# Moving the denominator step, the transposes and the query/key/value weight loads in a fused linear-attention and gated-FFN layer

## What is computed

```
qkv = x @ w_qkv;  q = elu(q) + 1;  k = elu(k) + 1;  kv = k * v
run_kv_f, run_ks_f = decay_scan(kv, a), decay_scan(k, a)      # out[t] = a*out[t-1] + in[t]
run_kv_s, run_ks_s = decay_scan(kv, b), decay_scan(k, b)
den_f = clip(sum_over_head(q * run_ks_f), 1e-6);  den_s = the same with run_ks_s
att = concat(q * run_kv_f / den_f, q * run_kv_s / den_s) @ w_out
y   = layernorm(x + att)
out = layernorm(y + (silu(y @ wg.T) * (y @ wu.T)) @ wd.T)     # wg, wu, wd: int32 / 127
```

## Time and profile before

| what | us |
|---|---|
| median of 3 runs | 2980.36 |
| lowest and highest of them | 2740.66, 2985.13 |
| the profiled execution | 2740.66 |
| its span on the slowest core | 2739.1 |
| spans of all cores | 2712.3 to 2739.1 |

### The profile page before, as it was taken

One profiled execution on the slowest core, in us unless ns is written; L12 is line 12 of the kernel. 1 busy time (PEld: TensorE's weight loads), 2 busy tenths in 40 slices (PEclk: granted clock), 3 DMA queues, 4 the chain that ended last, 5 costly groups with the idle time before them and its releaser, 6 DMA issues.

```text
span 2739.1 us, 21184 instructions; the slowest of 8 cores (2712.3 to 2739.1 us)
## 1 busy us (share of the span) xinstructions
PE 1753.3 (64%) x7153; PEld 726.9 (27%) x7298; DVE 833.9 (30%) x1010; ACT 525.3 (19%) x576; POOL 384.8 (14%) x308
## 2 busy tenths in 40 slices
PE   0222253788567883778567883778467883878586
PEld 0000011333222331333223331333123331333232
DVE  0122204342334313342334313342334313441111
ACT  0011102221113202221113212221123112221111
POOL 6411111111012101111021101111121101120000
PEclk9655567899888996899889996999789996999898
DMA  8999983424733273323633263323532273314433
GB/s 111 127 126 128 125 146 101 132 76 101 164 115 100 64 175 88 128 80 96 169 115 100 70 170 121 101 73 110 156 131 85 76 196 102 103 58 147 134 104 112
DMA packets 259467, 316.06 MB, mean 115 GB/s; under 512 B 91171, under 2 KB 173092, under 8 KB 257060
## 3 DMA queue, kind: packets, MB, share of 16 engines
q1 hardware_dynamic: 175396, 235.00, 29.4%
q0 software_dynamic: 7168, 46.15, 12.9%
q10 hardware_dynamic: 76800, 33.57, 5.7%
HBM read 318.80 MB, written 54.53 MB: 136 GB/s over the span
## 4 chain that ended last, share of the span: by engine, by line
PE 45%; DVE 16%; ACT 10%; DMA 8%; POOL 7%; issue 6%; another core or an unknown queue 6%; ACTq 1%; SPq 0%; DVEq 0%; POOLq 0%
DVE runs L529 11%; PE C_ps L722 8%; PE A_ps L391 8%; PE D_ps L722 6%; POOL denr L408 4%; DMA wo_buf<-wo_s 4%; PE C_ps L776 3%; PE D_ps L776 3%; PE A_ps L776 3%; PE B_ps L776 3%; POOL runs L551 3%; PE B_ps L391 2%; ACT sgb L732 2%; PE C_ps L599 2%
## 5 line engine op out<-in xcount | busy, mean ns | idle before, releaser
L722 PE MATMUL C_ps<-y1T,wg_buf 128*128 128x512 bf16 x1506 | 379.3, 406 | 202.6 <-ACT sgb L732 131.0
L391 PE MATMUL A_ps<-xT,wq_buf 128*128 128x512 bf16 x1003 | 280.2, 438 | 168.6 <-DMA wq_buf<-wq_s 132.9
L551 POOL TENSOR_TENSOR runs<-qb,runs 128x1024 f32<-128x1024 f32 x64 | 148.7, 2345 | 1420.2 <-DVE states_sb L538 1420.2
L722 PE MATMUL D_ps<-y1T,wu_buf 128*128 128x512 bf16 x1504 | 344.6, 379 | 3.4 <-DVE hbuf L739 0.3
L420 PE MATMUL B_ps<-denr,bones_sb 128*128 128x512 bf16 x124 | 57.3, 556 | 450.4 <-POOL denr L408 450.4
L739 DVE TENSOR_TENSOR hbuf<-D_ps,sgb 128x1024 bf16<-128x1024 f32 x96 | 117.6, 1225 | 562.7 <-ACT sgb L732 562.7
L722 PEld LDWEIGHTS C_ps<-y1T,wg_buf 128*128 128x128 bf16 x1536 | 152.5, 103 | 426.7 <-issue 284.7
L732 ACT ACTIVATE sgb<-C_ps,cv_sb 128x1024 bf16<-128x1024 f32 x96 | 107.0, 1114 | 565.2 <-PE D_ps L722 401.1
L391 PEld LDWEIGHTS A_ps<-xT,wq_buf 128*128 128x128 bf16 x1024 | 111.3, 111 | 341.6 <-issue 265.0
L722 PEld LDWEIGHTS D_ps<-y1T,wu_buf 128*128 128x128 bf16 x1536 | 149.0, 98 | 187.1 <-issue 10.0
L391 PE MATMUL B_ps<-xT,wq_buf 128*128 128x512 bf16 x504 | 124.9, 402 | 47.5 <-DMA wq_buf<-wq_s 47.0
(11 more groups left out here) (79 smaller groups left out, 1494.1 us busy)
## 6 DMA issues: line engine op xcount, KB each, us to landing
wq_buf<-wq_s SPq DMA_DIRECT2D x192, 256.0 KB, 3.6
wg_buf<-wg_s SPq DMA_DIRECT2D x192, 256.0 KB, 3.0
wu_buf<-wu_s SPq DMA_DIRECT2D x192, 256.0 KB, 4.3
wd_buf<-wd_s SPq DMA_DIRECT2D x384, 128.0 KB, 2.2
wo_buf<-wo_s SPq DMA_DIRECT2D x256, 128.0 KB, 3.5
out<-work ACTq DMA_DIRECT2D x64, 256.0 KB, 6.0
xbf<-x POOLq DMA_DIRECT2D x32, 256.0 KB, 185.6
xbm<-xbf POOLq DMA_DIRECT2D x32, 256.0 KB, 4.6
```

The costliest lines, as they stand in the source:

```text
L391: t.matmul(o, a, b, start=f1, stop=f2),
L551: lambda v, q_=qv, r_=kvpart: v.tensor_tensor(r_.rearrange("p (o t) -> p o t", o=2), q_, r_.rearrange("p (o t) -> p o t", o=2), OP.mult),
L722: t.matmul(o, a, b, start=f1, stop=f2),
```

## The change

1. `emit_den` moves out of `emit_A` to the level of the subtiles. A pair no longer runs its denominator step at the head of the next pair's segment; it is put into a list `den_q`, and `pop_den()` takes it from there: behind gate steps 2, 6 and 10 for pairs 0, 1 and 2, and between the two halves of stage D for pair 3. In stage A of subtile 0 it is called behind every second segment, which is the old order.
2. The call of `next` behind the additions of line 618 goes. The first two segments (matmuls of pair 0, scans of pair 0) come behind the whole first layer norm.
3. The loads of wq are issued by POOL (`q="gpsimd"`) and not by SP. The first three chunks stand ahead of the `xbm` loads.
4. The transposes of x and of y1 are issued by SP and not by ACT. Those of y1 come behind all of the layer norm, and the first chunks of wg and wu stand between the second and the third of them.
5. The waits of the second half of stage D on `A_ps` and `B_ps` are read when that half is emitted, so that they take in the denominator step of pair 3.

```diff
     def emit_A(sg):
         s, st = divmod(sg, NST)
+        for ci in range(3):
+            stream_chunk2(sg, "wq", wq_buf, wq_s, wq_in, wq_slot_g,
+                          wq_cval, ci, q="gpsimd")
         emit_xcast(sg)
         for c in range(NCH):
...
-            prog.op("scalar",
+            prog.op("sync",
                     lambda s_, d=dview, z=sview: s_.dma_start(
                         out=d, in_=z, transpose=True),
...
-        for ci in range(3):
-            stream_chunk2(sg, "wq", wq_buf, wq_s, wq_in, wq_slot_g,
-                          wq_cval, ci)
...
             if mi % 2 == 1 and ci + 3 < 12:
                 stream_chunk2(sg, "wq", wq_buf, wq_s, wq_in, wq_slot_g,
-                              wq_cval, ci + 3)
+                              wq_cval, ci + 3, q="gpsimd")
...
-        pend = [None]
         for pr in range(NJ // 2):
-            if pend[0] is not None:
-                emit_den(*pend[0])
-                pend[0] = None
...
-            pend[0] = (pr, qp, v_q, v_scans, num_vals)
+            den_q.append((pr, qp, v_q, v_scans, num_vals))
             yield
-        emit_den(*pend[0])
-        pend[0] = None
         g["xT"] = ch_m.n
-        yield
...
         g["xbm_v"] = ch_v.n
-        if a_next_gen is not None:
-            next(a_next_gen, None)
...
+        y1t_tr(2)
+        y1t_tr(3)
+        stream_chunk2(sg, "wg", wg_buf, wg_s, wg_in, wg_slot_g, wg_cval, 0)
+        stream_chunk2(sg, "wu", wu_buf, wu_s, wu_in, wu_slot_g, wu_cval, 0)
+        y1t_tr(0)
+        y1t_tr(1)
+        for ci in range(1, 3):
             stream_chunk2(sg, "wg", wg_buf, wg_s, wg_in, wg_slot_g,
                           wg_cval, ci)
...
             if mp in (1, 3, 5, 7, 9) and a_next_gen is not None:
                 next(a_next_gen, None)
+            if mp in (2, 6, 10):
+                pop_den()
...
             if h2 == 0:
                 gPS["C"] = [("v", ch_v.n)]
                 gPS["D"] = [("v", ch_v.n)]
+                pop_den()
+                if a_next_gen is not None:
+                    next(a_next_gen, None)
```

More of the change, by code:

```diff
@@ L290, in stream_chunk2 @@
         mi0 = 2 * ci
[L291 to L307, removed]
+        rdy = [conv_ready[key][mi0], conv_ready[key][mi0 + 1]]
+        assert all(r is not None for r in rdy), (key, mi0)
+        for a in range(2):
+            dst2 = buf[:, sl * 2048 + a * 1024: sl * 2048 + (a + 1) * 1024]
+            prog.op(q,
+                    lambda s, d=dst2, z=scratch[mi0 + a]:
+                        s.dma_start(out=d, in_=z),
+                    waits=rdy + [(ch_m, slot_g[sl])],
+                    inc=wch, inc_n=16)
         cval[ci] = (wch, wch.n)
@@ L354, in emit_xcast, with emit_den @@
         return ch_xc.n
+    def emit_den(pr, qp, v_q, v_scans, num_vals):
+        for jj in range(2):
+            j = 2 * pr + jj
+            qv = qb[qp][:, jj * 512:(jj + 1) * 512].rearrange(
+                "p (o t) -> p o t", o=1).broadcast_to([128, 2, 512])
+            kvpart = runs[:, jj * 2048: jj * 2048 + 1024]
+            kspart = runs[:, jj * 2048 + 1024: jj * 2048 + 2048]
+            v_dr = prog.op(
+                "gpsimd",
+                lambda v, q_=qv, r_=kspart: v.tensor_tensor(
+                    denr.ap().rearrange("p (o t) -> p o t", o=2), q_,
+                    r_.rearrange("p (o t) -> p o t", o=2), OP.mult),
+                waits=[(ch_v, v_scans), (ch_v, v_q),
+                       (ch_m, g["denr"])], inc=ch_p)
+            wB2 = [(chof(t), v) for t, v in gPS["B"]]
+            m_d = None
+            for dec in range(2):
+                m_d = prog.op(
+                    "tensor",
+                    lambda t, o=B_ps[:, dec * 512:(dec + 1) * 512],
+                    r_=denr[:, dec * 512:(dec + 1) * 512]:
+                        t.matmul(o, bones_sb[:], r_, start=True,
+                                 stop=True),
+                    waits=([(ch_p, v_dr)] + (wB2 if dec == 0 else [])),
+                    inc=ch_m if dec == 1 else None, inc_n=2)
+            g["denr"] = ch_m.n
+            v_cl = prog.op("vector",
+                           lambda v: v.tensor_scalar(
+                               denc[:], B_ps[:], 1e-6, None, OP.max),
+                           waits=[(ch_m, m_d), (ch_v, g["denc"])],
+                           inc=ch_v)
+            gPS["B"] = [("v", v_cl)]
+            v_ln = prog.op("scalar",
+                           lambda s_: s_.activation(denc[:], denc[:],
+                                                    AF.Ln),
+                           waits=[(ch_v, v_cl)], inc=ch_s)
+            v_ex = prog.op("scalar",
+                           lambda s_: s_.activation(
+                               denc[:], denc[:], AF.Exp,
+                               scale=cvap("neg1")),
+                           waits=[(ch_s, v_ln)], inc=ch_s)
+            num_val = num_vals[jj]
+            cview = concat.ap().rearrange(
+                "p (d e t) -> p d e t", d=2, e=NJ)[:, :, j, :]
+            v_of = prog.op(
+                "vector",
+                lambda v, o=cview, r_=kvpart: v.tensor_tensor(
+                    o, r_.rearrange("p (o t) -> p o t", o=2),
+                    denc.ap().rearrange("p (o t) -> p o t", o=2),
+                    OP.mult),
+                waits=[(ch_s, v_ex), (ch_m, g["concat"]),
+                       (ch_p, num_val)],
+                inc=ch_v)
+            g["denc"] = v_of
+            g["concat_ready"] = v_of
+        g["runs"] = ch_v.n
+        g_q[qp] = ch_v.n
@@ L681, in emit_BCD @@
                 g_stat[wl] = ch_v.n
[L682 to L692, removed]
         if a_next_gen is not None:
@@ L695, in emit_BCD, with y1t_tr @@
             next(a_next_gen, None)
-        for ci in range(3):
+        def y1t_tr(c):
+            dview = y1T.ap().rearrange("p (j t) -> p j t", j=NJ)[
+                :, :, c * 128:(c + 1) * 128]
+            sview2 = y1b[:, c * DM:(c + 1) * DM].rearrange(
+                "p (j f) -> p j f", j=NJ)
+            prog.op("sync",
+                    lambda s_, d=dview, z=sview2: s_.dma_start(
+                        out=d, in_=z, transpose=True),
+                    waits=[(ch_v, y1vals[c]), (ch_m, g["y1T"])],
+                    inc=ch_yt, inc_n=16)
+        y1t_tr(2)
[5 more added lines that the diff above has]
+        for ci in range(1, 3):
             stream_chunk2(sg, "wg", wg_buf, wg_s, wg_in, wg_slot_g,
@@ L701, in emit_BCD @@
                           wu_cval, ci)
+        yt_val = ch_yt.n
+        g["xbm_yt"] = ch_yt.n
         for mp in range(NMI_F // 2):
@@ L768, in emit_BCD @@
                     if k == 0 and c == 0:
-                        w = w + firstD[h2]
+                        keys = ("C", "D") if h2 == 0 else ("A", "B")
+                        w = w + [(ch_v, h_done)] + [
+                            (chof(t), v) for key in keys for t, v in gPS[key]]
                     prog.op(
@@ L865, in build_nc @@
     a_gen = emit_A(0)
-    run_gen(a_gen)
+    _SENT = object()
+    nseg = 0
+    while next(a_gen, _SENT) is not _SENT:
+        nseg += 1
+        if nseg % 2 == 0:
+            pop_den()
+    while den_q:
+        pop_den()
     for sg in range(N_SUBTILES):
```

13 lines of the change are left out of this document (8 added, 5 removed).

## The result

| | before | changed |
|---|---|---|
| median of 11 runs, us | 2806.73 | 2676.23 |
| lowest to highest | 2734.33 to 2985.13 | 2672.29 to 2951.17 |
| profiled execution | 2740.66 | 2674.31 |
| ratio, with 95% interval | 1 | 0.9776 (0.9761 to 0.9792) |

The change makes the kernel 2.2% faster. Some runs of both kernels are a few per cent longer than the rest, with a lower granted clock on some of the cores; the ratio leaves these out, and so does all that follows. The forecast was 2639, or 3.7% under the profiled execution of the kernel before: the sign is right, the time 35 us too low, inside the range of 2570 to 2725.

What follows compares the result with a forecast made beforehand. The prediction took the kernel to be bound by PE and its waits, chiefly 450.4 us for `denr`. It summed 2740.66 + 132 (start) - 234 (seven periods) = 2639 us, range 2570 to 2725.

Steps and rivals of the forecast that it cites:

- The start: Subtile 0: wq loads wait behind POOL's conversions, first matmul at 350, first wout ends at 541.6 and not 409.7: +132 us.
- Without SP's 9.4% the queue is 36 us shorter: At the start: POOL's queue, without SP's share beside it, runs dry at 348 and not 384.4 us.
- The period: Each of seven equal stretches after the first wout: 271.8 us against 305.2, 234 us gained over seven.
- wout to first gate step: In each period: 24 us, bounds 22 and 38, from transposes of x there at +14 and y1T at +20 to +24.
- gate steps 0 and 1: In each period: 6.9 + 2.6 (wait for Silu) + 6.9 = 16.4 us; scans end before gate step 1 needs `D_ps`.
- two middle segments: In each period: pair matmuls, gate step, denominator, three gate steps; 52.8 us each, 105.6 together, hardly less than before.
- last segment: In each period: ends at the product of gate step 11, which stage D waits for; 13.4 + 6.9 + 17.7 = 38.0 us.
- wait between them: Stage D, between its halves: the second half waits until `B_ps` is clipped twice; a new wait of 10.5 us.
- 192 matmuls, 41.5 + 1: Stage D, both halves, in each period: 42.5 us of matmuls.
- Loads served at once: Rival for the start: wq loads do not wait for the conversions; first matmul at 127, 2530 us in all; chance 0.11.
- Late transposes: Rival in each period: transposes of y1 pushed back on SP, first gate step at +38; 2737 us, no change; chance 0.15.
- Start not shortened: Rival: stage A of subtile 0 takes 289.4 us again after 350; 2784 us, 1.6% slower; chance 0.06.

Runs made afterwards that it cites:

- e1: The changed kernel, but in subtile 0 alone the loads of wq are issued by SP again, behind the transposes of x; 2557.45 us.
- e4: The changed kernel, but POOL issues the last 24 conversions of x (subtiles 2 to 7) behind stage A of subtile 0; 2658.74 us.
- e7: The changed kernel, but SP loads wq in every subtile, with the transposes of x and y1 staying on SP; 2633.94 us, ratio to before 0.960.
- e2_order_only: The changed kernel's new order, but all DMAs issued by the engines that issued them in the kernel before; 2737.15 us.
- e9_xt_early_den_c: New order, DMAs on old engines, stage A's loads called in the old place, pair 3's denominator step in `C_ps` inside stage D's second half; 2576.65 us.
- e5_den_c: The changed kernel, but pair 3's denominator step goes into `C_ps`, its halves inside the second half of stage D; 2629.34 us, ratio to before 0.951.
- e3_queues_only: The kernel before with only the moved queues (wq on POOL, transposes of x and y1 on SP), old order; 2847.3 us, ratio to before 1.037.

## Why the forecast was right in its sign and too low in its size

Two terms of the sum were too small, and they make up nearly all of the 35 us: the start by 13 us, stage D by 22 us over seven periods. The other terms of a period miss by up to 1.6 us each and cancel, which is luck.

**The start, +132 forecast, +145 measured.** The mechanism was right, and e1 and e4 show it: one queue, worked off in order, at 2.4 us a transfer. The term that was mis-sized is "Without SP's 9.4% the queue is 36 us shorter": the last conversion landed at 364.0 us (issued at 93.8, 270.2 to landing) and not at 348, so the queue became 20 us shorter, and the first matmul came at 367.0 and not 350. The last conversion of x (tile `xbf`) and the queues from 0 to 367 us, to be held against the earlier trace rows:

```profile
L235 POOL DMA_DIRECT2D xbf<-x x32: 493/940/1203, 1.6 to 93.8; - x32
...
DMA to landing us min/median/max: 2.8/8.0/270.2
```

```profile
q0 software_dynamic: 5263, 39.94, 94.4%
q1 hardware_dynamic: 5380, 1.87, 2.9%
```

POOL's queue (q0) did get most of the share, 94.4% against 85.7%, but it moved 39.94 MB in 367 us, 109 GB/s, against 101 before: 8% more, where a queue 36 us shorter needs 10%. Why a share of the engines moved less was not tested. Stage A then took 158.1 us (159.6 forecast) and wout 29.7 (32).

**The period, 271.8 forecast, 275.2 measured, 24 us over seven.** By pieces, from the starts and ends on PE's timeline, for the period from 1072.4 and at the mean of all seven (the wout is there the one that ends the period):

| piece | forecast | period from 1072.4 | mean of seven |
|---|---|---|---|
| wout | 32 | 31.9 | 32.4 |
| wout to first gate step | 24 | 23.5 | 24.6 |
| gate steps 0 and 1 | 16.4 | 18.1 | 17.9 |
| two middle segments | 105.6 | 103.5 | 104.0 |
| last segment | 38.0 | 37.2 | 37.3 |
| both halves of stage D | 42.5 | 45.7 | 45.7 |
| wait between them | 10.5 | 10.5 | 10.5 |
| last additions | 2.8 | 2.8 | 2.8 |

The step that failed is "192 matmuls, 41.5 + 1": they took 45.7 us, so the term was 3.2 too small, in each of the seven periods. I had taken the full clock, with nothing for the clock behind the standing that I had myself put in front of the second half (23.3 us where the kernel before takes 20.9), nor for the first half behind its wait for the last gate step (22.4). Before, the second half took 20.9 in each period, and the two together 42.6 to 42.8 in four of them and 44.1 in three. In gate steps 0 and 1 there were two things that I had not counted. In the period from 1072.4 gate step 1 waited 1.32 us for the product of gate step 0, which stands behind the scans on DVE; I had said that it would not. In four others a group of 16 matmuls took 5.1 to 5.3 us and not 3.6, behind a wait of 2.6 us.

**Right number, partly wrong reason.** I had the 24 us from the transposes of x, there at +14. They took 5.48 us to issue, not 13, and were there at +3.2 (1107.45). In the period shown what sets the first gate step is that ACT finishes the layer norm before it turns to Exp and Relu of k, so that the q matmuls wait 7.8 us for `kphi`. In the other six the transposes of y1 land 0.6 to 2.6 us later still, so both paths end at nearly the same time. The 13.04 us of the earlier trace rows were beside the output and the loads of wo.

**The rivals.** Loads served at once: refuted, by the first matmul at 367. The Trainium skill's sentence in "DMA: Bandwidth & Descriptors", section "Issuing engines are not separate DMA queues", that the issuing engine saves only issue time, does not hold here as a forecast of a kernel's time: moving the 24 loads of wq of subtile 0 to another issuing engine cost 145 us, for the ring order that the same page gives in "Queues, rings and completion order". Late transposes: in the changed kernel the transposes of y1 cost 8.4 us over seven periods and not 98; e7 shows how near it was, where 14 us a period appear once SP has one more stream. Start not shortened: refuted, a pair took 37 to 39 us.

**A wrong idea of my own afterwards.** In `e2_order_only` I expected the order to carry the gain alone. My sum had the term for the queues only as a matter of wout and wg; it did not say that item 2 moves the transposes of x behind the layer norm wherever the engine that issues them also computes it.

## What to carry to other kernels

- A queue is a place in an order, not a label. When a load is moved to another engine's queue, list everything that was put into it before, with the time at which that lands; here 144 conversions issued in 95 us kept it full for 364 us. A move that helps in the steady state can be left out of the first round alone.
- When code that is emitted in one piece is moved in the order, every DMA inside it moves too, on every engine; an engine that both computes and issues then issues late.
- Look for the PSUM tile that is free at the new place before moving a step there: in `B_ps` the step cost 10.5 us of standing and 2.4 us at a lower clock behind it, in `C_ps` 0.8 us for its own four matmuls (`e9_xt_early_den_c`), and 2.6 us more at the mean where the loads of wq met those of wd (`e5_den_c`).

## What the runs showed of the hardware that was not expected

Periods of identical work differ by some 20 us with the granted clock alone: 277.2 at 0.92 and 295.6 at 0.82 in `e1_wq0_sp`, and likewise one period in `e5_den_c` and two in `e3_queues_only`. Each time two neighbouring cores have the long period together and the others do not: cores 0 and 1 (301 and 295 us) and later 2 and 3 (293 and 296) in `e1_wq0_sp`, 4 and 5 (311 and 308, 317 and 316) in `e3_queues_only`, 6 and 7 (287 and 284) in `e5_den_c`. What sets off such a period stays open; no run here was made for it. Four transposes of x take 6.35 us to issue when nothing else is being moved (`e2_order_only`), 5.48 behind the last loads of wo, and 13.04 in the middle of wout beside the output.
